# A transformer block on one core: the values group of a step moved behind the last scores, to stand next to the denominators

## The chip, the cores and the metric

The kernel runs on one core of a Trainium2 chip. The metric is the device time of one execution in microseconds. Lower is better. The core's engines each work through their own list of instructions in order and wait for each other by semaphores. PE is TensorE, DVE is VectorE, ACT is ScalarE, POOL is GpSimd, and SP issues the DMAs.

## The reference

The input is x of 4 batches x 2048 tokens x 512 channels. The reference makes a modulation from a small vector, normalizes x, runs causal attention of 16 heads with 32 channels each, and adds the gated result to x:

```python
mod = (_silu(L0_c) @ L0_wmod).reshape(L0_c.shape[0], 6, 1, -1)
sa, ca, ga, sb, cb, gb = (mod[:, 0], mod[:, 1], mod[:, 2], mod[:, 3], mod[:, 4], mod[:, 5])
h = _layernorm(x, axis=-1) * (1 + ca) + sa
# in the attention:
qkv = x @ W_qkv + b_qkv
q = _apply_rope(q, cos, sin); k = _apply_rope(k, cos, sin)
att = jnp.einsum('bhqd,bhkd->bhqk', q, k) / jnp.sqrt(jnp.float32(HS))
att = jnp.where(causal, att, jnp.float32(-1000000000.0))
att = jax.nn.softmax(att, axis=-1)
y = jnp.einsum('bhqk,bhkd->bhqd', att, v)
x = x + ga * (y @ W_proj + b_proj)
```

A second part (layer norm, a routed attention with its own layer norm at the end) follows in the reference. The kernel takes as its inputs only the weights of the first part and the gain and shift of the last layer norm. Each token's row of the output is made from the attention's result by a product with the projection and two normalizations.

## The kernel before

The work of the attention is cut into 16 **stages**: 4 batches x 4 groups of four heads. A stage has two parts.

The **projection part** makes query, key and value of the *next* group: per tile of 128 tokens 12 products on PE (L1060), bias and rotation on DVE and POOL, and a transposition on PE (L1073).

The **step part** is the loop over 40 steps (L1200). A step `s` is a pair `STEPS[s] = (cq, kt)`: 512 query columns (`cq` 0 to 3) against one tile of 128 keys (`kt` from 0 to 4 cq + 3). The last four key tiles of each `cq` are on the diagonal; they are narrower (512, 384, 256, 128 columns) and get a mask product. A step issues on PE:

- four **scores** products, one for each head (L1119), each into one of three banks `ps_scores`. Each waits until ACT has made the exponential (L675) that frees its bank, which is that of three scores before.
- the **values** group of the step before (L1133): four products with 32 output columns each, one per head, into `ps_out`. It waits for all four exponentials of that step.
- the **denominators** of the step before: also groups of four products with 32 columns, into `ps_den`. On the diagonal they read the exponentials (L1156). Off it, POOL adds the exponentials of two steps (`add_pair`, L483) and a **pair-sum** group (L1150) reads the sum, once for two steps. In the last stage there are no pairs, and each step has a group on L1156.
- up to five **maxima** products (`unit_scores`, L1083, with a mask product L1086 on the diagonal): scores of the *next* stage, of which DVE takes the row maxima (L844), so that the exponentials there have their shift. They go through three banks, the `ring`, which also takes the products with the output projection (`proj`, L1105) and the transposed tiles of the next batch (`head_turn`, L1036). A product into the ring waits until DVE has emptied the bank of three uses before.

How many maxima products stand in a step is fixed in advance by `unit_plan`, from a table of loads of PE and DVE. The order within a step is written out by hand in the loop over `place` 0 to 4: scores `place`, then, at certain places, values and denominators, then maxima product `place`. The other engines follow the same loop over steps. ACT makes four exponentials per step, each of which also waits until its `prob` buffer has been used (`prob_used`, three steps deep). ACT also copies finished sums out, and at such times it waits for DVE's reciprocals (L860) and POOL's product (L488). DVE has, between the maxima, the reciprocals, the tiles of the output (`tail_stage`) and the normalizations of the next batch's input (L716, L723, L793). In the last stage nothing comes after, so there are no maxima products, and the output tiles of its own batch are made in it.

`late` is step 1 of a stage that has a next one: there values and denominators come at place 4, after the last tiles' transpositions. Behind a step with `kt` = 0, which opens new sums, values come at place 3. In the other steps they come at place 2.

Of the kernel before, what the change touches and what calls it, by code (L numbers as in the profile page):

```python
# [24 lines left out]
def adaln_block_kernel(nc, x, w_qkv, b_qkv, w_proj, b_proj, ln_g, ln_b, c, w_mod, rope_cos, rope_sin, out):  # L25
# [24 lines left out]
    STEPS = [(cq, kt) for cq in range(NC_) for kt in range(TPC * (cq + 1))]  # L50
# [35 lines left out]
    def tail_at(g, first, last):  # L86
        if first:
            return {}
        if g < 2:
            return {s: g * T0 + k for k, s in enumerate((2, 8, 16, 24, 30))}  # L90
        if g == (2 if last else 3):
            return {s: 2 * T0 + k for k, s in enumerate((2, 8, 14, 20, 26, 30))}
        return {}

    def head_at(g, last):
        return HEAD_AT if g == 2 and not last else {}

    def own_at(g, last):
        return OWN_AT if g == NG - 1 and last else {}
# [19 lines left out]
    def unit_plan(tail, head):  # L119

        fits = lambda r: [min(5, max(0, r * product_load(s, tail, head) - vector_load(s, tail, head))) for s in range(NS)]
        r = 0.0
        while sum(fits(r)) < NS * HG:
            r += 0.01
        plan, k, done = [], 0, 0.0
        for room in fits(r):
            done += room
            upto = min(NS * HG, k + 5, int(done + 0.5))
            plan.append([(i // HG, i % HG) for i in range(k, upto)])
            k = upto  # L130
        assert k == NS * HG
        return plan
# [7 lines left out]
    with ExitStack() as ctx:  # L140
# [125 lines left out]
        def ring_base(b):  # L266

            return NS * HG if isinstance(b, int) and b == 0 else NS * HG + RING * b - NT

        def ring_first(b):  # L270

            return ring_base(b if isinstance(b, int) and b == 0 else 1) % NBK
# [748 lines left out]
        def _(pe):  # L1021
# [10 lines left out]
            def head_turn(b, t, use, n):  # L1032
                pe.wait_ge(head_norm, NT * b + t + 1)
                pe.wait_ge(ring_free, wait_value(use - NBK + 1))
                for k in range(KC):
                    mm = pe.transpose(ring[n % NBK][:, k * P:(k + 1) * P], wk[:, t % 2, k * P:(k + 1) * P], ident[:])  # L1036
                mm.then_inc(ring_full, 1)

            def turn_maxima(G):
                pe.wait_ge(max_split, G + 1)  # L1040
                pe.transpose(ring[0][:, 0:P // 2].bitcast(F16), nm16[:].rearrange("p a n -> p (a n)"),
                             ident16[:]).then_inc(max_turned, 1)

            def qkv(G, g, before, loads):
                pe.wait_ge(wg_ld[g % 2], loads)
                if before is not None:
                    pe.wait_ge(sums_left, NC_ * (before - 1) + NC_)
                for t in range(NT):
                    qkv_tile(G, g, t)
                    if t == 1 and before is not None:  # L1050
                        turn_maxima(before)
                    if t >= 3:
                        turn_tile(G, t - 3)
# [11 lines left out]
            def turn_tile(G, t):  # L1065
                N = NT * G + t
                pe.wait_ge(lo_done, N + 1)
                pe.wait_ge(hi2_done, N + 1)
                pe.wait_ge(tr_evac, wait_value(N - 1))
                for two in range(2):  # L1070
                    for h in range(HG):
                        o = (two * HG + h) * P
                        mm = pe.transpose(ps_tr[t % 2][0:R, o:o + P], qk16[:, t % 3, h, two * R:(two + 1) * R],  # L1073
                                          ident16[:])
                mm.then_inc(qk_tr, 1)
# [34 lines left out]
            def scores(G, par, s, h):  # L1110

                cq, kt = STEPS[s]
                q0 = P * max(kt - TPC * cq, 0)
                w = QC - q0
                diag = kt >= TPC * cq
                k = HG * s + h

                pe.wait_ge(exp_done, wait_value(HG * NS * G + (k - NBK + 1 if k >= NBK else 0)))
                mm = pe.matmul(ps_scores[k % NBK][:, 0:w], qk[0:RM, par, 1, h, kt * P:(kt + 1) * P],  # L1119
                               qk[0:RM, par, 0, h, cq * QC + q0:(cq + 1) * QC], start=True, stop=not diag)  # L1120
                if diag:
                    mm = pe.matmul(ps_scores[k % NBK][:, 0:P], identb[:], mask_kq[:], start=False, stop=True)  # L1122
                mm.then_inc(scores_done, 1)

            def values(G, par, s, paired):

                cq, kt = STEPS[s]
                q0 = P * max(kt - TPC * cq, 0)
                if kt == 0:
                    pe.wait_ge(sums_left, wait_value(NC_ * G + cq))  # L1130
                pe.wait_ge(exp_done, HG * (NS * G + s + 1))
                for h in range(HG):
                    mm = pe.matmul(ps_out[h * HS:(h + 1) * HS, q0:QC], v32[:, par, kt, h * HS:(h + 1) * HS],  # L1133
                                   prob[:, s % 3, h // 2, h % 2, 0:QC - q0], start=kt == 0,
                                   stop=kt == TPC * (cq + 1) - 1)
                if kt < TPC * cq and paired:
                    mm.then_inc(prob_used, 1)
# [39 lines left out]
            def body(b, first, last):  # L1177
                base = ring_base(b)
                n = 0
                bank0 = ring_first(b)  # L1180
                for g in range(NG):
                    G = NG * b + g
                    par = g % 2
                    nxt = not (last and g == NG - 1)
                    if nxt:
                        if g == NG - 1:
                            pe.wait_ge(head_done, NT * (b + 2))

                        qkv(G + 1, (g + 1) % NG, G, 32 * (NG // 2 * b + (g + 1) // 2 + 1))
                        first_evac = NT * (G + 2) - NBK  # L1190
                    else:
                        turn_maxima(G)
                        first_evac = None
                    pe.wait_ge(max_rows, G + 1)
                    pe.wait_ge(max_dma, 32 * (G + 1))
                    if g == 0:
                        pe.wait_ge(scale_rows, 1)
                    tail, head, own = tail_at(g, first, last), head_at(g, last), own_at(g, last)
                    plan = unit_plan(tail, head)
                    for s in range(NS + 1):  # L1200

                        units = plan[s] if s < NS and nxt else []
                        late = s == 1 and nxt
                        for place in range(5):
                            if place < 4 and s < NS:
                                if s == 0 and place < NBK and first_evac is not None:
                                    pe.wait_ge(qkv_evac, first_evac + place + 1)
                                scores(G, par, s, place)
                            if (s, place) in LATE_TURNS and nxt:
                                turn_tile(G + 1, LATE_TURNS[s, place])  # L1210
                            if place == 4 and late:
                                pe.wait_ge(tr_evac, NT * (G + 2))
                            if place == (4 if late else 3 if s > 1 and STEPS[s - 1][1] == 0 else 2) and s > 0:
                                values(G, par, s - 1, nxt)
                            if place == (4 if late else 3) and s > 0:
                                denominators(G, s - 1, nxt)
                            if place < len(units):
                                u, h = units[place]
                                unit_scores(h, u, 1 - par, base + n, bank0 + n)
                                n += 1  # L1220
                        if s in tail or s in own:
                            proj(b if s in own else b - 1, own[s] if s in own else tail[s], base + n, bank0 + n)
                            n += 1
                        if s in head:
                            head_turn(b + 1, head[s], base + n, bank0 + n)
                            n += 1
                return n + bank0
# [43 lines left out]
```

## Time and profile before

| | |
|---|---|
| time, median of 3 runs | 3621.95 us (3618.25 to 3622.92) |
| span of the profiled execution | 3618.4 us (no other time of its own is given) |
| PE busy | 3195.3 us, 88% |
| DVE busy | 2923.3 us, 81% |
| ACT, POOL busy | 1780.1 and 1710.6 us |
| granted TensorE clock, mean | 0.952 |

Busy time is the union of an engine's instructions. A PE product is shown until its results have arrived, so products that follow each other overlap in the rows, and the rate of PE is read from one start to the next. The groups of four products with 32 columns are 8 rows of MATMUL each, since the type is f32, and the timeline merges them to one row with x8. PEld is the load of a product's weights, which stands ahead of it in the queue; it can wait while PE is still busy with earlier products.

### The profile page before, as it was taken

The numbers are of one execution on the slowest core, as the hardware profiler recorded it, in microseconds if no ns is written. First come the engines' busy times: TensorE is split into PE (matmuls) and PEld (weight loads), VectorE is DVE, ScalarE is ACT, GpSimd is POOL, SyncE is SP. The second block draws the span as 40 slices with busy tenths as digits, with TensorE's granted clock in tenths as the row PEclk, the third lists the DMA queues.
The fourth block names the chain that finished last, engine by engine and source line by source line (L and its number), as shares of the span: only waits on it lengthen the run. The fifth ranks groups of instructions, "written<-read, shape, count | busy, mean of one in ns | idle before, by whom it ended". The sixth has DMA issues, their size and how long they took to land.

```text
span 3618.4 us, 69458 instructions
## 1 busy us (share of the span) xinstructions
PE 3195.3 (88%) x22176; PEld 1266.8 (35%) x22176; DVE 2923.3 (81%) x5670; ACT 1780.1 (49%) x3667; POOL 1710.6 (47%) x1385
## 2 busy tenths in 40 slices
PE   3699999999989989888988989989888999999895
PEld 1324343424343332434334243333424334243221
DVE  4797777897778888898878878888888888888676
ACT  3306565555645454564535545465444545544451
POOL 2403435373526455373653626455363554626454
PEclk8759999999999999999999999999999999999897
DMA  6000000110011000110111001010011010001022
GB/s 213 12 12 4 18 8 7 35 36 15 10 41 40 24 25 27 30 42 21 40 33 41 31 18 42 27 31 25 27 42 47 30 36 21 27 19 36 19 91 73
DMA packets 112229, 124.62 MB, mean 34 GB/s; under 512 B 18276, under 2 KB 85092, under 8 KB 110708
## 3 DMA queue, kind: packets, MB, share of 16 engines
q1 hardware_dynamic: 111864, 120.07, 10.5%
q8 instruction: 190, 3.11, 0.4%
q14 instruction: 175, 1.43, 0.1%
HBM read 83.02 MB, written 36.50 MB: 33 GB/s over the span
## 4 chain that ended last, share of the span: by engine, by line
PE 40%; DVE 31%; issue 13%; DVEq 6%; ACT 2%; POOLq 2%; POOL 2%; DMA 0%; ACTq 0%; SPq 0%
PE ring L1083 10%; DVE mpart L844 9%; PE ps_out L1133 9%; PE ps_scores L1119 7%; PE ps_den L1150 4%; DVE qk L821 4%; PE ps_den L1156 3%; PE ring L1105 3%; DVE wk L888 3%; DVE qk L807 2%; DVE ropeB L829 2%; DVE qk L816 2%; PE ps_scores L1060 2%; DVE dsum L860 2%; DVEq L838 1%
## 5 line engine op out<-in xcount | busy, mean ns | idle before, releaser
L675 ACT ACTIVATE prob<-ps_scores 128x512 f32<-128x512 f32 (+3 forms) x2560 | 1265.7, 537 | 1105.7 <-PE ps_scores L1122 535.0
L844 DVE TENSOR_REDUCE mpart<-ring 128x1 f32<-128x512 f32 (+3 forms) x2560 | 1403.0, 599 | 335.0 <-PE ring L1086 181.7
L483 POOL TENSOR_TENSOR psum<-prob 128x1024 f32<-128x1024 f32 x360 | 866.8, 2429 | 325.5 <-ACT prob L675 163.0
L1083 PE MATMUL ring<-qk 96*128 96x512 f16 (+3 forms) x2560 | 892.3, 368 | 118.1 <-DVE mpart L844 106.3
L1119 PE MATMUL ps_scores<-qk 98*128 98x512 f16 (+3 forms) x2560 | 879.2, 357 | 57.5 <-ACT prob L675 53.6
L1133 PE MATMUL ps_out<-prob,v 128*32 128x512 f32 (+3 forms) x5120 | 609.4, 548 | 6.6 <-ACT qk L635 6.6
L1083 PEld LDWEIGHTS ring<-qk 96*128 96x128 f16 x2560 | 239.7, 99 | 943.8 <-DVE mpart L844 704.4
L1060 PE MATMUL ps_scores<-wg,hT 128*128 128x384 f16 x3072 | 538.3, 328 | 22.9 <-ACT osum L702 9.9
L465 POOL TENSOR_TENSOR ropeA<-qk,cos_sb 128x256 f32<-128x256 f32 x256 | 200.5, 783 | 750.1 <-DVE v L810 745.2
L1119 PEld LDWEIGHTS ps_scores<-qk 98*128 98x128 f16 x2560 | 248.4, 99 | 364.0 <-ACT prob L675 232.9
L1060 PEld LDWEIGHTS ps_scores<-wg,hT 128*128 128x128 f16 x3072 | 292.2, 98 | 200.7 <-issue 18.9
L630 ACT CAST qk<-qk 128x128 f16<-128x128 f32 x256 | 76.2, 298 | 378.1 <-DVE qk L816 378.1
L860 DVE RECIPROCAL dsum<-dsum 128x128 f32<-128x128 f32 x252 | 234.7, 937 | 18.9 <-ACT osum L702 17.6
L1086 PE MATMUL ring<-mask_qk,identb 128*128 128x128 bf16 x1024 | 233.2, 230 | 0.0
L1122 PE MATMUL ps_scores<-mask_kq,identb 128*128 128x128 bf16 x1024 | 229.6, 226 | 0.0
L1105 PE MATMUL ring<-wp,otin 128*128 128x512 f16 x756 | 187.7, 399 | 41.6 <-DVE mpart L844 28.0
L1156 PE MATMUL ps_den<-prob,ones 128*32 128x512 f32 (+3 forms) x2240 | 216.8, 459 | 0.0
L1150 PE MATMUL ps_den<-psum,ones 128*32 128x512 f32 x1440 | 208.5, 620 | 2.2 <-POOL psum L483 2.2
L513 POOL TENSOR_TENSOR x<-wk,xs 128x512 f32<-128x512 f32 x48 | 61.3, 1277 | 309.1 <-DVE wk L873 309.1
L807 DVE SCALAR_TENSOR_TENSOR qk<-ps_scores,bg 128x256 f32<-128x256 f32 x256 | 108.8, 425 | 98.5 <-PE ps_scores L1060 57.9
L821 DVE TENSOR_TENSOR qk<-qk 128x128 f16<-128x128 f32 x256 | 179.4, 701 | 1.2
L453 POOL TENSOR_TENSOR vare<-mv,eps_t 128x1 f32<-128x1 f32 x192 | 54.5, 284 | 245.3 <-DVE mv L718 89.8
(127 smaller groups left out, 3134.9 us busy)
## 6 DMA issues: line engine op xcount, KB each, us to landing
xs<-in_L_attn_x_dram SPq DMA_DIRECT2D x124, 256.0 KB, 2.8
attn_out_T<-ot SPq DMA_DIRECT2D x63, 256.0 KB, 2.2
otin<-attn_out_T SPq DMA_DIRECT2D x30, 512.0 KB, 4.6
out_dram<-x SPq DMA_DIRECT2D x60, 256.0 KB, 2.1
wg<-w_qkv_halves SPq DMA_DIRECT2D x16, 768.0 KB, 5.2
qk<-in_L_wmod_dram SPq DMA_DIRECT2D x1, 6144.0 KB, 27.1
bc<-modulation SPq DMA_DIRECT2D x4, 1536.0 KB, 9.1
hT<-in_L_attn_W_qkv_dram SPq DMA_DIRECT2D x1, 3072.0 KB, 10.4
```

Source lines behind the costliest of these rows:

```text
L483: pool.tensor_tensor(psum2[:, p], prob[:, s % 3, p], prob[:, (s + 1) % 3, p], ALU.add).then_inc(pair_sum, 1)
L675: act.activation(prob[:, s % 3, p, h % 2, 0:w], ps_scores[(HG * s + h) % NBK][:, 0:w], ACT.Exp, scale=SCALE).then_inc(exp_done, 1)
L821: dve.tensor_tensor(qk16[:, u, :, 2 * HS:3 * HS], ropeR[:, u, :, 0, :], qk16[:, u, :, 0:HS], ALU.subtract)
L844: dve.tensor_reduce(mpart[:, h, qt, kc:kc + 1], ring[n % NBK][:, 0:w], AX.X, ALU.max).then_inc(ring_free, 1)
L860: dve.reciprocal(dsum[:, cols], dsum[:, cols]).then_inc(recip_done, 1)
L1060: mm = pe.matmul(ps_scores[(t + SHIFT) % NBK][:, 0:GW], hT[:, a, k, t * P:(t + 1) * P], wg[:, g % 2, w, k, :], start=(i == 0), stop=(i == ...
L1083: mm = pe.matmul(ring[n % NBK][:, 0:w], qk[0:R, par, 0, h, qt * P:(qt + 1) * P], qk[0:R, par, 1, h, kc * QC:kc * QC + w], start=True, stop ...
L1105: mm = pe.matmul(ring[n % NBK][:, :], att, wp16[:, w, k, :], start=(i == 0), stop=(i == 3 * NG - 1))
L1119: mm = pe.matmul(ps_scores[k % NBK][:, 0:w], qk[0:RM, par, 1, h, kt * P:(kt + 1) * P], qk[0:RM, par, 0, h, cq * QC + q0:(cq + 1) * QC], st ...
L1133: mm = pe.matmul(ps_out[h * HS:(h + 1) * HS, q0:QC], v32[:, par, kt, h * HS:(h + 1) * HS], prob[:, s % 3, h // 2, h % 2, 0:QC - q0], start ...
L1150: mm = pe.matmul(ps_den[h * HS:(h + 1) * HS, :], ones[:], psum2[:, h // 2, h % 2, :], start=kt == 2, stop=False)
L1156: mm = pe.matmul(ps_den[h * HS:(h + 1) * HS, q0:QC], ones[:], prob[:, s % 3, h // 2, h % 2, 0:QC - q0], start=kt == 0, stop=kt == TPC * (c ...
```

## The change

The values group is called at the place of the denominators, directly ahead of them, in all steps: place 3, or place 4 in the late step.

```diff
@@ -1210,9 +1210,8 @@
                                 turn_tile(G + 1, LATE_TURNS[s, place])
                             if place == 4 and late:
                                 pe.wait_ge(tr_evac, NT * (G + 2))
-                            if place == (4 if late else 3 if s > 1 and STEPS[s - 1][1] == 0 else 2) and s > 0:
+                            if place == (4 if late else 3) and s > 0:
                                 values(G, par, s - 1, nxt)
-                            if place == (4 if late else 3) and s > 0:
                                 denominators(G, s - 1, nxt)
                             if place < len(units):
                                 u, h = units[place]
```

PE's list in step 27 of a stage with maxima products (third group of a batch in the loop over batches), before. L1119 is scores, L1083 a maxima product, L1133 values, L1150 pair sums; `psum2` holds the sums of pairs:

```order
L1083 MATMUL ring0<-qk 128x512 [waits ring_free]
L1118 REGISTER_ALU
L1119 MATMUL ps_scores2<-qk 128x512 [waits exp_done]
L1131 ISA
L1133 MATMUL ps_out<-prob,v32 32x512 [waits exp_done]
L1133 MATMUL ps_out<-prob,v32 32x512 x3
L1082 REGISTER_ALU
L1083 MATMUL ring1<-qk 128x512 [waits ring_free]
L1118 REGISTER_ALU
L1119 MATMUL ps_scores0<-qk 128x512 [waits exp_done]
L1149 ISA
L1150 MATMUL ps_den<-psum2,ones 32x512 [waits pair_sum]
```

The same place on PE with the change:

```order
L1083 MATMUL ring0<-qk 128x512 [waits ring_free]
L1118 REGISTER_ALU
L1119 MATMUL ps_scores2<-qk 128x512 [waits exp_done]
L1082 REGISTER_ALU
L1083 MATMUL ring1<-qk 128x512 [waits ring_free]
L1118 REGISTER_ALU
L1119 MATMUL ps_scores0<-qk 128x512 [waits exp_done]
L1131 ISA
L1133 MATMUL ps_out<-prob,v32 32x512 [waits exp_done]
L1133 MATMUL ps_out<-prob,v32 32x512 x3
L1149 ISA
L1150 MATMUL ps_den<-psum2,ones 32x512 [waits pair_sum]
```

The third maxima product and the fourth scores product now stand ahead of the values group, which stands directly ahead of the pair sums.

PE's list in steps 28 and 29 of the last stage, which has no maxima products, before:

```order
L1119 MATMUL ps_scores1<-qk 128x512 [waits exp_done]
L1119 MATMUL ps_scores2<-qk 128x512 [waits exp_done]
L1119 MATMUL ps_scores0<-qk 128x512 [waits exp_done]
L1133 MATMUL ps_out<-prob,v32 32x512 [waits exp_done]
L1133 MATMUL ps_out<-prob,v32 32x512 x3
L1119 MATMUL ps_scores1<-qk 128x512 [waits exp_done]
L1156 MATMUL ps_den<-prob,ones 32x512 x4
```

The same with the change:

```order
L1119 MATMUL ps_scores1<-qk 128x512 [waits exp_done]
L1119 MATMUL ps_scores2<-qk 128x512 [waits exp_done]
L1119 MATMUL ps_scores0<-qk 128x512 [waits exp_done]
L1119 MATMUL ps_scores1<-qk 128x512 [waits exp_done]
L1133 MATMUL ps_out<-prob,v32 32x512 [waits exp_done]
L1133 MATMUL ps_out<-prob,v32 32x512 x3
L1156 MATMUL ps_den<-prob,ones 32x512 x4
```

Here the four scores products follow each other without anything between them. DVE, ACT, POOL and SP have the same lists as before.

## Rows read from the trace of the kernel before

**Rows 1.** The page: busy shares of the engines, and the chain that ended last.
```profile
PE 3195.3 (88%) x22176; PEld 1266.8 (35%) x22176; DVE 2923.3 (81%) x5670; ACT 1780.1 (49%) x3667; POOL 1710.6 (47%) x1385
...
PE 40%; DVE 31%; issue 13%; DVEq 6%; ACT 2%; POOLq 2%; POOL 2%; DMA 0%; ACTq 0%; SPq 0%
```

**Rows 2.** Windows (PE, PEld, DVE, ACT, POOL busy): plain, product, head step part; last stage.
```profile
483.00:627.00 144.00, 137.31 (x1025) 46.52 (x1026) 106.52 (x193) 89.24 (x181) 66.34 (x33) 0.99 0.03 9
1275.00:1448.00 173.00, 154.98 (x1084) 54.57 (x1084) 143.92 (x238) 89.38 (x182) 97.04 (x68) 0.98 0.08 27
1490.00:1656.00 166.00, 147.37 (x1090) 55.38 (x1088) 150.44 (x306) 99.64 (x198) 97.46 (x81) 0.99 0.10 30
3415.00:3618.00 203.00, 162.38 (x1052) 48.89 (x1050) 129.56 (x188) 80.98 (x171) 89.55 (x103) 0.88 0.24 75
```

**Rows 3.** Waits (total, times, longest) in the product and the head step part.
```profile
PEld ring L1083 <- DVE mpart L844: 43.9, 58, 3.1
PE ring L1083 <- DVE mpart L844: 8.5, 11, 2.2
...
PEld ring L1083 <- DVE mpart L844: 43.8, 60, 2.2
PE ring L1083 <- DVE mpart L844: 10.9, 14, 1.7
```

**Rows 4.** Timeline of PE (start, duration): plain stage, steps 27, 28; a values-denominators join.
```profile
578.44 1.06 PE L1133 MATMUL ps_out<-prob,v 128*32 128x512 f32 x8
579.44 0.39 PE L1083 MATMUL ring<-qk 96*128 96x512 f16 x1
...
580.98 0.60 PE L1083 MATMUL ring<-qk 96*128 96x512 f16 x2
...
582.15 0.39 PE L1083 MATMUL ring<-qk 96*128 96x512 f16 x1
582.38 0.38 PE L1119 MATMUL ps_scores<-qk 98*128 98x512 f16 x1
582.69 1.06 PE L1133 MATMUL ps_out<-prob,v 128*32 128x512 f32 x8
583.69 0.39 PE L1083 MATMUL ring<-qk 96*128 96x512 f16 x1
583.92 0.60 PE L1119 MATMUL ps_scores<-qk 98*128 98x512 f16 x2
...
1500.91 1.06 PE L1133 MATMUL ps_out<-prob,v 128*32 128x512 f32 x8 [0.47 <-ACT qk L635]
1501.79 1.05 PE L1156 MATMUL ps_den<-prob,ones 128*32 128x512 f32 x8
```

**Rows 5.** Timeline of PE, last stage: step 13 (kt before is 0), step 14.
```profile
3453.02 0.81 PE L1119 MATMUL ps_scores<-qk 98*128 98x512 f16 x3
3454.09 0.39 PE L1119 MATMUL ps_scores<-qk 98*128 98x512 f16 x1 [0.26 <-ACT prob L675]
...
3456.27 0.82 PE L1119 MATMUL ps_scores<-qk 98*128 98x512 f16 x3
...
3459.34 0.39 PE L1105 MATMUL ring<-wp,otin 128*128 128x512 f16 x1
```

**Rows 6.** Timeline of DVE in the plain stage beside rows 4.
```profile
577.25 0.69 DVE L844 TENSOR_REDUCE mpart<-ring 128x1 f32<-128x512 f32 x1 [0.69 <-PE ring L1083]
...
580.71 3.18 DVE L844 TENSOR_REDUCE mpart<-ring 128x1 f32<-128x512 f32 x5
```

**Rows 7.** Timelines of PE and DVE in a head stage, steps 27 and 28.
```profile
1603.14 0.39 PE L1083 MATMUL ring<-qk 96*128 96x512 f16 x1 [0.21 <-DVE x L793]
...
1604.68 0.60 PE L1083 MATMUL ring<-qk 96*128 96x512 f16 x2
...
1606.49 0.39 PE L1083 MATMUL ring<-qk 96*128 96x512 f16 x1 [0.99 <-DVE mpart L844]
...
1604.95 0.94 DVE L860 RECIPROCAL dsum<-dsum 128x128 f32<-128x128 f32 x1
```

## The prediction

> **What bounds the kernel now.** I read the page's shares first [rows 1]: PE is busy 88% of 3618.4 us and DVE 81%, ACT, POOL and DMA far less, and the chain that ended last is 40% PE, 31% DVE and 13% "issue", so two engines share the bound and the question is which has it where. The windows by stage [rows 2] answer that. A stage is one group of four heads; it has a projection part, which the change leaves alone, and a step part, which it touches. I name the step parts by what DVE has beside its row maxima:
> - plain (3 of the 16): 144 us, PE 137.3 busy, DVE 106.5: PE alone sets the pace;
> - product (9): 173 us and more, PE 155.0, DVE 143.9: now one, now the other;
> - head (3): 166 us, PE 147.4, DVE 150.4: mostly DVE;
> - the last one: 203 us with the end of the kernel, no maxima.
>
> The waits [rows 3] say the same. The weight load of a maxima product stands still for DVE 43.9 us in a product and 43.8 us in a head stage, but PE itself was idle for it only 8.5 and 10.9 us. The difference is what other PE work, the values group among it, covers. That cover is what the change moves.
>
> **What the change removes: switches of PE.** Values, pair sums and denominators are groups of four products with 32 output columns; all else on PE here has 128. The start-to-start times in [rows 4] give the price of going from one to the other. Maxima to scores, both with 128 output columns, is 0.23 us (582.15 to 582.38). Scores to a values group is 0.31 (582.38 to 582.69). A values group to a product with 128 output columns is 1.00 (582.69 to 583.69). A values group to a denominators group right behind it is 0.88 (1500.91 to 1501.79). So going in costs about 0.31 - 0.22 = 0.09 us (two scores in a row are 0.22 apart: the row at 583.92 holds two, 0.60 us together and 0.38 each) and coming out 1.00 - 0.88 = 0.12, and a join of two groups saves one of each: 0.21 us.
>
> The Trainium skill has two rules on it that do not agree. "TensorEngine Tiling (Array Packing)", section Key Properties, says that a change of tiling mode drains the engine; "TensorE: Matmul & The Clock Gate", section Step-by-step, says that the next matmul's fill overlaps the drain of the one before, so that a stream costs its columns alone. By the second there is nothing to save in a switch and the sum below has only its losses. The rows speak for the first, with 0.09 and 0.12 us.
>
> **How many joins.** Of the 40 steps of a stage, the first keeps its place, and so do the three behind a step with kt = 0, and the closing call has nothing between its two groups. That leaves 35 moved values groups. In 15 stages denominators of key tiles off the diagonal are made from pair sums, once in two steps, so only 23 of the 35 have a group to join (14 on the diagonal, 9 with a pair alone). The other 12 only move past one scores and one maxima product. In the last stage there are no pairs, the step after the first moves too, and all 36 join. 15 x 23 + 36 = 381 joins, 381 x 0.21 = 80 us, 2.2% of the span, if nothing stood against it. No wait is added; the semaphores are those of before. But PE goes through its list in order, so a maxima or scores product that has to wait now holds up values and denominators, which used to run in that time.
>
> **The cover that goes, last stage.** Between scores 2 and scores 3 there is nothing left there, and scores 3 needs the bank that exponential 0 of its own step frees. The trace has this order already, in the steps behind kt = 0 [rows 5]: scores 0 to 2 at 3453.02, scores 3 only at 3454.09, idle for ACT, then values and denominators joined, next step at 3456.27: 3.25 us. The next step, in the old order, goes from 3456.27 to 3459.34: 3.07 us. So a wide step loses 0.40 us of cover for a join of 0.21, and is 0.18 us longer. With some 24 wide steps, and nothing for the narrow ones (a shorter exponential, a shorter cover), this is +4.5 us; I take +5. Ends: 0, if the product tiles between the steps keep setting the time, and +10, if the joins give nothing there (24 x 0.40).
>
> **Plain stages.** [Rows 4] begin in a step with a pair group, the next has none, and [rows 6] are DVE beside them. The third maxima product comes at 579.44, 1.00 us behind values at 578.44. In the new order it stands where values stood, at 578.35 since it needs no switch; its bank was freed by the maximum that ended at 577.94. Scores 3 follow at 578.57, values at 578.88, pair sums at 579.76 and the fourth maxima product at 580.76, where it was 580.98. The join pays in full. In the following step the second maxima product (582.15) waited for DVE already and stays where it is. The third could go at 582.60 and needs the bank of the one issued behind 580.98; its maximum is the third in DVE's unbroken row of five of 0.64 us each, so the bank is free at about 582.7. Values go near 583.2, where they were at 582.69, but the third maxima and scores 3 are then behind PE, and the next step, which began at 584.14 with the second product of the row at 583.92, begins at about 584.2. The gain of 0.22 is gone. Not every step is that full. So of 23 x 0.21 = 4.8 us I keep half: -2.4 per stage, -7 for three. Ends -4.8 and +1 each.
>
> **Head stages.** In [rows 7] PE has the third maxima product at 1603.14, idle 0.21 us for DVE although the values group went right before it. In the new order it still waits for 1603.14 and nothing hides that: PE stands for some 1.3 us. Scores 3 follow at 1603.37, values at 1603.68, pair sums at 1604.56, and the fourth maxima product comes at 1605.56 where it was 1604.68, 0.88 us late. But DVE reaches that one only after its reciprocal (1604.95 + 0.94) and the third maximum, and at 1606.49 PE was idle 0.99 us for DVE anyway. The lateness ends there. With one of 16 tiles in every second step I take this for 20 of 23 joins: nothing lost, nothing won, 0 per stage. Ends: -4.8, and +10 if the 0.73 us of a mean wait (43.8 / 60) less the 0.21 is lost in each of the 20.
>
> **Product stages.** Five or six tiles, with two to three steps of heavy DVE work each, so about 11 of the 23 joins stand as in the head stages (0) and 12 as in the plain ones (0.10 each): -1.2, for nine -11. Ends -4.8, and +6 if the 0.76 us of a mean wait (43.9 / 58) less 0.21 is lost in each of 11.
>
> **Sum.** -7 + 0 - 11 + 5 = -13 us. This is against the profiled execution, whose span of 3618.4 us is the only time of its own that is given, within the 3618.25 to 3622.92 of the timed runs. So it is within their scatter, what lies around the span adds nothing that can be told, and I take the difference from the median: 3622 - 13 = 3609 us. By the rule that a drain costs nothing only the +5 of the lost cover would be left, 3627; with the 0.31 and the 1.00 against 0.88 in the rows I give that no chance of its own.
>
> **Rivals.**
> - DVE takes it all. For it: DVE is 81% busy over the whole and 91% in the head stages, and the number of maxima per step is fixed by a plan that the change does not touch. Against it: 74% in a plain stage (106.5 of 144). The joins give nothing but in a few narrow steps, and 3620 us comes out, no change.
> - The cover is worth more than the switch. A maxima or scores product that waits now keeps values and denominators standing in its queue, and the time is not given back by a later wait that shrinks. The place is the third maxima product of steps in product and head stages. The upper ends above make 9 x 6 + 3 x 10 = 84 us of lateness. It decides the sign once a quarter of that survives to the next values group (13 + 7 us against 84); with a third of it, 28 us, +5 in the last stage and nothing won elsewhere it is 3655 us. For it: the gain lost again in [rows 4, 6]; a longer block of 2.2 us without a maxima product, against three banks of 0.69 us each. Against it: the wait at 1606.49.
> - The joins are paid nearly in full, -50 us, 3572 us, if DVE, which gets its third tile a microsecond earlier, frees banks earlier too. Against it: its order of work is fixed and it is already behind where it is waited for.
> - TensorE's clock: the windows of [rows 2] have a granted clock of 0.98 to 0.99 and the last stage 0.88, a mean over the upper level of 2.4 GHz and the lower of 1.2. PE now stands still for longer at a time in some steps, and each 10 us that it works at the lower level instead of the upper cost 5. I give it no case of its own; it is one reason for a wide range.
>
> **How the numbers follow.** This kernel's measurement can tell about 0.2%, 7 us, from no change. Forecast (the joins pay in part, 3609) 0.40; DVE takes it 0.22; cover lost 0.32; nearly full gain 0.06. The forecast's own range is 3590 to 3618, and about a tenth of its chance is too small to tell. With the full gain, faster is 0.42; same 0.26; slower 0.32. The range takes in most of the lost cover and half of the full gain: 3572 to 3655.
>
> **What would show it.** Right: pair-sum and denominators groups start 0.88 us behind values groups; a plain step part is 2 to 3 us shorter than 144, a head part the same within 2 us, wide steps of the last stage 3.25 us. Wrong: PE's own idle time for DVE at the maxima line doubles in product and head stages and their step parts grow (cover lost); a join that costs 1.00 us as before (no saving); plain parts unchanged with DVE waits on PE in them grown.

## The result

The changed kernel takes 3627.5 us (median of 20 runs, 3620.2 to 3634.9) against 3622.6 us before (20 runs, 3617.5 to 3626.7). The ratio is 1.0017, with a 95% interval of 1.001 to 1.0023: slower by 0.17%, some 5 us. The forecast was 3609 us.

The page of the changed kernel, busy shares and the chain that ended last, to lay beside [rows 1]:

```profile
PE 3149.2 (87%) x22176; PEld 1315.1 (36%) x22176; DVE 2912.4 (80%) x5670; ACT 1754.9 (48%) x3667; POOL 1708.2 (47%) x1385
...
PE 38%; DVE 32%; issue 13%; DVEq 6%; ACT 3%; POOLq 2%; POOL 2%; DMA 0%; ACTq 0%; SPq 0%
```

PE is busy 46 us less in a span that is 5 us longer. So the joins did save time on PE, and more than that went into waits. The mean granted clock is 0.952 in both, which hides that it went down in some stages and up in others. The windows say where. Those of the changed kernel run from the end of one projection part to the start of the next (plain, product, head), under them the same windows of the kernel before (columns as in [rows 2]):

```profile
478.40:617.20 138.80, 133.11 (x1027) 50.54 (x1026) 105.22 (x194) 87.92 (x182) 66.31 (x33) 0.99 0.03 9
1262.70:1439.30 176.60, 155.41 (x1087) 57.99 (x1084) 144.04 (x239) 88.55 (x182) 96.89 (x68) 0.96 0.08 27
1481.20:1648.60 167.40, 144.43 (x1091) 58.51 (x1088) 148.10 (x306) 98.49 (x198) 97.52 (x81) 0.99 0.09 30
```
```profile
482.60:626.90 144.30, 137.52 (x1027) 46.45 (x1026) 106.92 (x194) 89.54 (x182) 66.34 (x33) 0.99 0.03 9
1274.70:1448.10 173.40, 155.28 (x1087) 54.59 (x1086) 144.32 (x239) 89.72 (x182) 97.04 (x68) 0.98 0.08 27
1490.00:1656.50 166.50, 147.37 (x1090) 55.38 (x1088) 150.58 (x306) 100.13 (x198) 97.46 (x81) 0.99 0.10 30
```

The plain stage is 5.5 us shorter, the product stage 3.2 longer, with a granted clock of 0.96 for 0.98, and the head stage 0.9 longer. Summed over all 16, from the first scores product of a stage to that of the next: plain -15.1, head +2.6, product +19.2, last stage with the end of the kernel -2.7 us, and +1.4 ahead of the first. The -2.7 is mostly not the change's: the last stage is 1.7 to 3.1 us shorter also in the traces of experiments 1 and 3 that leave it as it was.

**The join.** In a plain stage of the changed kernel (PE, start and duration) values come at 570.43, pair sums 0.88 us later, the next maxima 0.98 after that:

```profile
569.90 0.38 PE L1083 MATMUL ring<-qk 96*128 96x512 f16 x1
570.12 0.38 PE L1119 MATMUL ps_scores<-qk 98*128 98x512 f16 x1
570.43 1.07 PE L1133 MATMUL ps_out<-prob,v 128*32 128x512 f32 x8
571.31 1.04 PE L1150 MATMUL ps_den<-psum,ones 128*32 128x512 f32 x8
572.29 0.61 PE L1083 MATMUL ring<-qk 96*128 96x512 f16 x2
...
573.69 0.38 PE L1119 MATMUL ps_scores<-qk 98*128 98x512 f16 x1
574.06 0.39 PE L1083 MATMUL ring<-qk 96*128 96x512 f16 x1
574.29 0.38 PE L1119 MATMUL ps_scores<-qk 98*128 98x512 f16 x1
```

**The step that lost.** Step 21 of a product stage, PE, of the changed kernel. Its first scores product (scores 0) stands at 1350.06:

```profile
1351.13 0.22 PE L1122 MATMUL ps_scores<-mask_kq,identb 128*128 128x128 bf16 x1
1354.28 0.45 PE L1083 MATMUL ring<-qk 96*128 96x512 f16 x1 [2.93 <-DVE mpart L844]
1354.52 0.53 PE L1119 MATMUL ps_scores<-qk 98*128 98x384 f16 x1
1354.84 0.31 PE L1122 MATMUL ps_scores<-mask_kq,identb 128*128 128x128 bf16 x1
1355.09 1.93 PE L1133 MATMUL ps_out<-prob,v 128*32 128x512 f32 x8
1356.80 1.58 PE L1150 MATMUL ps_den<-psum,ones 128*32 128x512 f32 x8
1358.20 1.03 PE L1156 MATMUL ps_den<-prob,ones 128*32 128x512 f32 x8
1359.16 0.39 PE L1083 MATMUL ring<-qk 96*128 96x512 f16 x1
```

and DVE there:

```profile
1350.83 2.68 DVE L888 SCALAR_TENSOR_TENSOR wk<-wk,rstd,bc 128x512 f32<-128x512 f32 x1
1353.66 2.08 DVE L844 TENSOR_REDUCE mpart<-ring 128x1 f32<-128x384 f32 x4 [0.15 <-issue]
1359.59 0.69 DVE L844 TENSOR_REDUCE mpart<-ring 128x1 f32<-128x512 f32 x1 [3.85 <-PE ring L1083]
```

The same step before, PE (scores 0 at 1363.17):

```profile
1367.32 0.39 PE L1083 MATMUL ring<-qk 96*128 96x512 f16 x1 [1.87 <-DVE mpart L844]
...
1367.86 1.06 PE L1150 MATMUL ps_den<-psum,ones 128*32 128x512 f32 x8
1368.74 1.04 PE L1156 MATMUL ps_den<-prob,ones 128*32 128x512 f32 x8
1369.72 0.60 PE L1083 MATMUL ring<-qk 96*128 96x512 f16 x2
```

The third maxima product goes 4.2 us into the step in both kernels, since DVE is held by L888 of an output tile. Before, values lay within that wait. Now they lie behind it, in front of pair sums *and* denominators, since the key tile of step 20 is the first on the diagonal. Two things follow. DVE has taken all that was there and stands 3.85 us for the next maxima product, so nothing gives the lateness back. And the groups take 1.71 and 1.40 us where a join takes 0.88: behind the unbroken wait PE works at the lower clock. The windows of step 21 in the six product stages with five tiles, of the changed kernel, tell the two apart (columns as above; the clock is third from the right):

```profile
1133.13:1141.12 7.99, 4.99 (x44) 1.90 (x41) 5.55 (x7) 1.85 (x4) 2.97 (x2) 1.00 0.09 31
1350.06:1359.61 9.55, 6.62 (x44) 2.18 (x41) 5.48 (x7) 1.85 (x4) 2.90 (x2) 0.82 0.27 82
2013.11:2024.03 10.92, 7.92 (x43) 2.27 (x40) 5.53 (x7) 1.85 (x4) 2.96 (x2) 0.69 0.06 21
2232.16:2240.09 7.93, 4.99 (x44) 1.91 (x41) 5.49 (x7) 1.85 (x4) 2.91 (x2) 1.00 0.32 101
2887.20:2897.88 10.68, 7.90 (x44) 2.22 (x40) 5.40 (x7) 1.92 (x4) 2.83 (x2) 0.68 0.05 19
3105.56:3114.45 8.89, 6.39 (x44) 2.07 (x41) 5.13 (x7) 1.92 (x4) 2.55 (x1) 0.81 0.26 79
```

Before, all six have a clock of 1.00 and 6.86 to 7.07 us, 41.8 in all, as these two do:

```profile
1363.17:1370.16 6.99, 5.12 (x41) 1.77 (x40) 5.41 (x7) 2.35 (x5) 2.83 (x2) 1.00 0.37 112
2017.94:2025.01 7.07, 5.12 (x42) 1.78 (x40) 5.49 (x7) 2.35 (x5) 2.91 (x2) 1.00 0.08 30
```

Now they are 56.0. Where the clock stays up, the step costs 0.9 us more. Where part of it is at 1.2 GHz, 2.0 to 3.9. The wait of PE ahead of the third maxima product is 2.50 to 3.00 us in the six, and 3.00 and 2.94 us in the two that keep the clock, so its length alone does not tell which step loses it.

### The profile page after: what moved, and what is told of

It is laid out like the page before. It is cut to its first block, busy times and chain, and to the rows that moved or that the text cites. A ratio compares the mean times of both kernels' runs of the same rounds, so it can differ in the third digit from the quotient of the medians.

```text
span 3623.7 us, 69458 instructions
## 1 busy us (share of the span) xinstructions
PE 3149.2 (87%) x22176; PEld 1315.1 (36%) x22176; DVE 2912.4 (80%) x5670; ACT 1754.9 (48%) x3667; POOL 1708.2 (47%) x1385
## 4 chain that ended last, share of the span: by engine, by line
PE 38%; DVE 32%; issue 13%; DVEq 6%; ACT 3%; POOLq 2%; POOL 2%; DMA 0%; ACTq 0%; SPq 0%
DVE mpart L844 10%; PE ring L1083 9%; PE ps_out L1133 9%; PE ps_scores L1119 6%; DVE qk L821 4%; PE ps_den L1150 3%; PE ring L1105 3%; PE ps_den L1156 3%; DVE wk L888 3%; DVE qk L807 2%; DVE ropeB L829 2%; DVE qk L816 2%; PE ps_scores L1060 2%; DVE dsum L860 2%; DVE wk L886 2%
## 5 line engine op out<-in xcount | busy, mean ns | idle before, releaser
L675 ACT ACTIVATE prob<-ps_scores 128x512 f32<-128x512 f32 (+3 forms) x2560 | 1239.0, 539 | 1098.1 <-PE ps_scores L1122 531.2
L844 DVE TENSOR_REDUCE mpart<-ring 128x1 f32<-128x512 f32 (+3 forms) x2560 | 1391.3, 598 | 355.1 <-PE ring L1086 184.4
L1083 PE MATMUL ring<-qk 96*128 96x512 f16 (+3 forms) x2560 | 890.6, 368 | 159.2 <-DVE mpart L844 115.2
L1119 PE MATMUL ps_scores<-qk 98*128 98x512 f16 (+3 forms) x2560 | 880.4, 356 | 77.3 <-ACT prob L675 71.1
L1133 PE MATMUL ps_out<-prob,v 128*32 128x512 f32 (+3 forms) x5120 | 613.8, 552 | 5.8 <-ACT qk L635 5.8
L1083 PEld LDWEIGHTS ring<-qk 96*128 96x128 f16 x2560 | 236.5, 99 | 810.5 <-DVE mpart L844 556.8
L1119 PEld LDWEIGHTS ps_scores<-qk 98*128 98x128 f16 x2560 | 251.5, 99 | 384.8 <-ACT prob L675 225.8
L1150 PE MATMUL ps_den<-psum,ones 128*32 128x512 f32 x1440 | 208.2, 619 | 0.0
```

The lines of the kernel that those rows point to most:

```text
L675: act.activation(prob[:, s % 3, p, h % 2, 0:w], ps_scores[(HG * s + h) % NBK][:, 0:w], ACT.Exp, scale=SCALE).then_inc(exp_done, 1)
L844: dve.tensor_reduce(mpart[:, h, qt, kc:kc + 1], ring[n % NBK][:, 0:w], AX.X, ALU.max).then_inc(ring_free, 1)
L1083: mm = pe.matmul(ring[n % NBK][:, 0:w], qk[0:R, par, 0, h, qt * P:(qt + 1) * P], qk[0:R, par, 1, h, kc * QC:kc * QC + w], start=True, stop ...
L1150: mm = pe.matmul(ps_den[h * HS:(h + 1) * HS, :], ones[:], psum2[:, h // 2, h % 2, :], start=kt == 2, stop=False)
```

## Experiments

All are measured beside the kernel before, on the same chip. Ratios are to before, with their 95% intervals.

**1. The change in one kind of stage alone.** One condition differs; that of the plain stages:

```diff
-if place == (4 if late else 3 if s > 1 and STEPS[s - 1][1] == 0 else 2) and s > 0:
+if place == (4 if late else 3 if (nxt and not tail and not head) or (s > 1 and STEPS[s - 1][1] == 0) else 2) and s > 0:
     values(G, par, s - 1, nxt)
```

Plain stages:

> The change in the three plain stages alone. The per-step comparison of the two traces has 5.0 us less in each of them (step part and the boundary behind it), so 3622 - 15 = 3607 us, if stages add up. Rival: what the plain stages gain is given back at the boundary or in the stages behind them, 3618 us or more.

Measured: 3610.3 us, ratio 0.9965 (0.9953 to 0.9977), so -12 us.

Product stages (`3 if tail or ...`):

> The change in the product stages alone (those with output tiles of the batch before). If the loss sits there: slower by 15 to 22 us, 3637 to 3644 us, more than the whole change. Rival (loss spread over all stages, or in the head and the last stage): within 5 us of before.

Measured: 3636.6 us, 1.0035 (1.0021 to 1.0048), +14 us.

Last stage (`3 if not nxt or ...`):

> The change in the last stage alone: 0.19 us more in each wide step and 0.07 in each narrow one, 3.7 us: 3626 us. The traces of before and of the change differ there by -1.6 us, since three stretches at the lower clock are missing in the change; if that comes from the order of the last stage and not by chance, it is 3621 us.

Measured: 3625.0 us, 1.0004 (0.9995 to 1.0013): +2 us, which is not told from none. Its wide steps have the pattern and the 3.26 us that was read off [rows 5]; here step 14 of the changed kernel, with its product tile from 3466.80:

```profile
3463.54 0.82 PE L1119 MATMUL ps_scores<-qk 98*128 98x512 f16 x3
3464.62 0.39 PE L1119 MATMUL ps_scores<-qk 98*128 98x512 f16 x1 [0.26 <-ACT prob L675]
3464.94 1.07 PE L1133 MATMUL ps_out<-prob,v 128*32 128x512 f32 x8
3465.82 1.04 PE L1156 MATMUL ps_den<-prob,ones 128*32 128x512 f32 x8
3466.80 2.76 PE L1105 MATMUL ring<-wp,otin 128*128 128x512 f16 x12
```

The parts add up to +7 us (-12 + 14 + 2, and the head stages' 2.6), and the whole is +5, so they add up within what such sums can tell. The loss is in the product stages.

**2. The lossy steps alone put back.** The change, with values at place 2 in two steps of each product stage (the edit is shown against the kernel before):

```diff
+if place == (4 if late else 2 if tail and s in ((21, 35) if g < 2 else (19, 35)) else 3) and s > 0:
     values(G, par, s - 1, nxt)
```

> The whole change, but in two steps of each product stage (21 and 35, or 19 and 35 in those with six tiles) values stay at place 2. Theory 1 (in these steps the third maxima product waits 2 to 3 us for DVE, values used to fill that wait, and PE's clock falls in the unbroken wait): 18 of some 700 calls moved back give 20 to 28 us: 3600 to 3607 us. Rival (waits of DVE's long operations would move to the next step): 3620 us or more.

Measured: 3604.8 us, 0.9949 (0.9935 to 0.9962). Eighteen calls out of the 561 that the change moves turn +5 us into -18. In its trace fifteen of them do it; in step 35 of the three stages with six tiles nothing comes back (+4.5 us against before, +4.1 in the change), and 6 says why.

**3. The clock apart from the cover.** The change, with eight products more in the same steps, ahead of the third maxima product. Their results are overwritten by scores 3.

```diff
+if place == 2 and tail and nxt and s in ((21, 35) if g < 2 else (19, 35)):
+    k3 = HG * s + 3
+    pe.wait_ge(exp_done, wait_value(HG * NS * G + k3 - NBK + 1))
+    for _ in range(8):
+        pe.matmul(ps_scores[k3 % NBK][:, :], qk[0:RM, par, 1, 3, 0:P],
+                  qk[0:RM, par, 0, 3, 0:QC], start=True, stop=True)
 if place < len(units):
```

> The whole change, with eight extra scores products in steps 19, 21 and 35 of the product stages, into the bank that scores 3 overwrites, right behind scores 2. They fill 1.7 of the 3.0 to 3.4 us in which PE waits there, add nothing to the result, and keep PE at work. If a good part of the change's loss in these steps is PE's clock at its lower level behind the wait (0.93 us lost in step 21 where the clock stays up, 2.0 to 3.9 us where it falls): 3610 to 3617 us, and step 21 longer than before by 0.9 us in all six stages. If it is the lost cover alone: 3627 us or more.

Measured: 3596.0 us, 0.9926 (0.9912 to 0.9939). Work that nobody needs makes the changed kernel 31 us faster, more than either expectation. Step 21 of the same stage, PE (L1221 are the extra products):

```profile
1348.83 1.89 PE L1221 MATMUL ps_scores<-qk 98*128 98x512 f16 x8
1351.97 0.39 PE L1083 MATMUL ring<-qk 96*128 96x512 f16 x1 [1.24 <-DVE mpart L844]
...
1352.51 1.06 PE L1133 MATMUL ps_out<-prob,v 128*32 128x512 f32 x8
1353.39 1.04 PE L1150 MATMUL ps_den<-psum,ones 128*32 128x512 f32 x8
1354.25 1.04 PE L1156 MATMUL ps_den<-prob,ones 128*32 128x512 f32 x8
```

The maxima product still goes 4.3 us into the step; the groups are back at 0.88 and 0.86. All six windows of step 21 have a clock of 1.00 and 7.6 to 8.0 us, 47.1 in all, and the two in which the change had kept its clock without them took 7.99 and 7.93, so the extra products do nothing there but hold the clock. So of the 14.1 us that the change lost in step 21, 5.2 are the cover (47.1 - 41.8, 0.9 a step) and 8.9 the clock. Step 19 gives back 5.8 us and step 35 of the stages with five tiles 10.7, with the clock at 1.00 there too. Not all of the 31 us is the clock, however: 5.7 come from step 35 of the stages with six tiles, where the clock was up already. That is a second thing, under 6.

The same products in the order of before, behind values and ahead of the third maxima product:

> The order of before with the same eight extra products in steps 19, 21 and 35 of the product stages, behind the values group and ahead of the third maxima product, where PE waits 2 us more. The clock is at its lower level in step 35 of five of the nine product stages of before; if the extra products keep it up there: 5 x 1.5 = 8 us less, 3614 us, and the change with them (3596) is 18 us ahead of it: that is what joining is worth with the clock alike. If the extra products helped the change in another way than by the clock (pair sums of POOL pushed past DVE's long operations), it is 3605 us or less.

Measured: 3603.1 us, 0.995 (0.9936 to 0.9964). The expectation had given 3605 us or less to another way than the clock. The trace does not show that way: DVE's long operations are as before (L888 takes 2.69 us and L934 0.75 on median in both). It shows the clock, at more places than I had counted. Steps 35 and 36 together of one product stage, before and with the extra products:

```profile
1423.44:1434.73 11.29, 9.11 (x51) 2.75 (x50) 9.17 (x13) 4.60 (x9) 6.88 (x4) 0.85 0.00 1
```
```profile
1421.32:1431.04 9.72, 9.37 (x59) 3.23 (x58) 9.05 (x13) 4.60 (x9) 6.55 (x4) 1.00 0.01 2
```

In all nine product stages it is so: a clock of 0.85 to 0.87 and 105.6 us before, 1.00 and 91.6 us now. The product stages as a whole get 12 us shorter, and 5 more go in other stages, where nothing was altered. With the extra products in both, the change is ahead by about 7 us, not by the 18 that I expected. This pair ran on two chips and its intervals just touch.

**4. Which cover is it?** Three orders of the same pieces, each shown by its main lines. `usual` is true in the late step, in step 1 of the last stage and behind a step with `kt` = 0, which keep their order. Joined between the third maxima product and scores 3 (scores 3 keeps its cover, the maxima product does not):

```diff
     unit_scores(h, u, 1 - par, base + n, bank0 + n); n += 1    # place 2
+if place == 2 and not usual:
+    values(G, par, s - 1, nxt)
+    denominators(G, s - 1, nxt)
```

> Joined groups between the third maxima product and scores 3: only scores 3 keeps its cover. Theory 1: the losses of 1 to 3.9 us at steps 19, 21 and 35 of product stages stay, the last stage gains 36 x 0.21 = 7 us instead of losing 5; about 3615 to 3622 us. Theory 2: as fast as with both covers, 3580 to 3590 us.

Measured: 3654.2 us, 1.0097 (1.0082 to 1.0111). Joined behind scores 3, the third maxima product behind the groups:

```diff
+for k in ([place] if usual else {2: [], 3: [2, 3]}.get(place, [place])):   # after values and denominators
```

> Joined groups behind scores 3 and ahead of the third maxima product: only the maxima product keeps its cover. Theory 1: the losses at steps 19, 21 and 35 of the product stages are gone, but two maxima products now follow each other behind the block; 3595 to 3605 us, wide steps of the last stage 3.25 us as in the change. Theory 2: as slow as the change, 3622 to 3630 us.

Measured: 3630.6 us, 1.0027 (1.0017 to 1.0037). Values alone moved behind the third maxima product, nothing joined:

> Only the values group moves, behind the third maxima product and ahead of scores 3, denominators stay behind scores 3: no join, the maxima product's cover gone, that of scores 3 kept. Theory 1: slower than the change by what the joins gave, 15 to 30 us: 3640 to 3655 us, plain stages no shorter than before. Theory 2: as fast as before, 3622 us. Theory 3: same as the change but for the last stage, about 3620 us.

Measured: 3687.3 us, 1.0185 (1.0172 to 1.0198).

In the product stages, against before and counted as above, the sums with joined groups are: +19 us with neither covered (the change), +26 with scores 3 covered (e2), -18 with the maxima product covered (e3), -33 with both (5 below). Uncovered and unjoined it is +44 (e4). So it is the maxima product's cover, worth 37 us in the change's order, while covering scores 3 alone wins nothing. All three totals missed what was expected all the same. In e3 the head stages got 25 us longer. e2 is 27 us behind the change and e4 60, and both have less of the clock (granted mean 0.943 and 0.946 for 0.952): over the span that is up to 34 and 25 us, by an estimate from these means. What is left of e4's 60 us, 35 or more, is 0.09 us or more for each of 381 joins, so it does not show that a join is worth more than 0.21. Why these orders have more stretches at the lower clock was not tried.

**5. Both groups at place 2.** The join and both covers:

```diff
-if place == (4 if late else 3) and s > 0:
+if place == (4 if late else 3 if s > 1 and STEPS[s - 1][1] == 0 else 2) and s > 0:
     denominators(G, s - 1, nxt)
```

> Values and denominators joined, but at place 2, ahead of the third maxima product and scores 3, so that the join is kept and both covers too. Theory 1 (the change lost its gain because the third maxima product waits for DVE with values, pair sums and denominators queued behind it): clearly faster than before, 381 joins x 0.21 us = 80 us at most, about 40 us after what DVE takes back: 3582 us, and no step of a product stage longer by over 0.6 us. Theory 2 (the loss is scores 3 waiting for ACT): the same here, faster by 25 to 50 us. Theory 3 (a join saves less than 0.21 us in this place): 3615 us or more. If the pair sums are not ready yet at place 2, waits of the pair-sum group for POOL appear, and the gain is halved.

Measured: 3622.0 us, 1.0002 (0.999 to 1.0014), single runs from 3605 to 3635. The expectation failed as a total. Product stages get 33 us shorter, head stages 39 longer. To see if it is the order in the head stage itself:

> Both groups at place 2 in the three head stages alone. The trace with both at place 2 everywhere has 12 to 15 us more in each head stage: 3661 us if that is the order in the head stage itself, DVE's normalization (L723) longer on mean than 0.87 us, since it runs beside POOL's pair sums. If it came from the stages ahead: 3622 us.

Measured: 3655.4 us, 1.0092 (1.0076 to 1.0107). It is. From scores 0 of step 0 to scores 0 of step 39 the third head stage of this kernel takes 174.9 us for 161.6, with a clock of 0.95 for 0.99, and its normalizations on DVE are longer; the window, then the row of L723 there, which had 903 ns on mean before:

```profile
2377.98:2552.93 174.95, 145.42 (x1038) 57.30 (x1037) 152.59 (x296) 96.03 (x191) 98.25 (x81) 0.95 0.10 28
...
L723 DVE TENSOR_SCALAR wk<-xs,mv,rstd 128x512 f32<-128x512 f32 x16 | 20.3, 1269 | 0.3 <-POOL rstd L455 0.2
```

That is 5.8 us of DVE's time and some stretches at the lower clock. Which of the two starts the other wasn't tried.

**6. Each stage in the order that suits it.** Plain stages as in the change, product stages with both groups at place 2, head and last stage as before:

```diff
+if place == (4 if late else 3 if (nxt and not tail and not head) or (s > 1 and STEPS[s - 1][1] == 0) else 2) and s > 0:
     values(G, par, s - 1, nxt)
+if place == (4 if late else 2 if tail and nxt and s > 1 and STEPS[s - 1][1] != 0 else 3) and s > 0:
     denominators(G, s - 1, nxt)
```

> Each kind of stage with the order that was best for it: plain as in the change, product with both groups joined at place 2, head and last stage as before. If the parts add up: -15 (plain), -33 (product), 0 (head, last): 3574 us. Rival: stages are coupled through the clock and POOL, and half is lost: 3598 us.

Measured: 3568.7 us, 0.985 (0.9835 to 0.9865): 54 us faster than before and the best version of all.

A side effect of the order shows in step 35 of product stages with six tiles. It is 1.3 to 1.4 us longer in the change at the full clock, and there PE has no wait for DVE ahead of the third maxima product. DVE of the changed kernel, then POOL:

```profile
1854.18 0.75 DVE L932 SCALAR_TENSOR_TENSOR wk<-wk,mv,bc 128x512 f32<-128x512 f32 x1
1855.00 2.67 DVE L934 SCALAR_TENSOR_TENSOR x<-wk,rstd,xs 128x512 f32<-128x512 f32 x1
...
1854.68 5.19 POOL L483 TENSOR_TENSOR psum<-prob 128x1024 f32<-128x1024 f32 x2 [1.20 <-PE ps_den L1150]
```

and the same with the extra products:

```profile
1847.93 0.75 DVE L934 SCALAR_TENSOR_TENSOR x<-wk,rstd,xs 128x512 f32<-128x512 f32 x1
...
1848.64 2.34 POOL L483 TENSOR_TENSOR psum<-prob 128x1024 f32<-128x1024 f32 x1 [2.23 <-PE ps_den L1150]
```

Before, it was the other of the two that was long:

```profile
1860.02 2.61 DVE L932 SCALAR_TENSOR_TENSOR wk<-wk,mv,bc 128x512 f32<-128x512 f32 x1
1862.71 0.75 DVE L934 SCALAR_TENSOR_TENSOR x<-wk,rstd,xs 128x512 f32<-128x512 f32 x1
```

The same DVE operation takes 0.75 us, or 2.67 when POOL's addition has started before it. The Trainium skill, "SBUF — State Buffer", section Who interferes with whom, has it that a VectorE instruction with two SBUF inputs contends with a GpSimd instruction that reads SBUF, and that the order of issue decides who blocks. The rows agree. Scores 3, 1.4 us earlier in the change, bring POOL's additions earlier, and they then meet L934, and L886 of the step before (2.56 us for 0.74), in place of L932. Of L886, L888, L932 and L934 three are slowed where it was two.

## Why the prediction was wrong

- **A join saves 0.21 us: right.** In the join above pair sums stand 0.88 us behind values, where values ahead of a product with 128 output columns take 1.00 [rows 4]. And from step 2 on each of the three plain stages is 4.1 to 4.3 us shorter for its 23 joins, 0.18 each. By the second of the two rules that the prediction took from the Trainium skill ("TensorE: Matmul & The Clock Gate", section Step-by-step: fill and drain overlap) there would have been nothing. That the sum by this rule was 3627, and 3627 was measured, is chance: the joins did pay, and the product stages lost it elsewhere.
- **Plain stages -7 us, upper end of the gain -4.8 each: too cautious.** -15.1 by the traces, -12 measured alone. I had worked out one pair of steps in which the gain is taken back, and halved the whole by it. In the changed kernel the next step does wait a little in such a place (from 573.69 to 574.06 it is 0.37 us, for 0.23 in the pair behind it), but the joins pay 0.18 of the 0.21 us on the mean. The rest of the 15.1 is 1.3 to 1.4 us each in steps 0 and 1 of two stages, which hold a stretch at the lower clock at another place than before; the third has nothing there. So 12.4 us are the joins.
- **Head stages 0: right** within 1 us each (+0.9). The third maxima product goes uncovered and a later wait takes it up. The sign that was named for lost cover, PE's idle time for DVE at the maxima line doubled, did not show in the product stages either (8.5 us in the window before, 10.3 in the change): it is a sum, and the loss sits in few steps.
- **Last stage +5: the mechanism right to 0.01 us, the sum not told from 0.** 0.19 us more in a moved wide step and 0.07 in a narrow one, wherever the clock is alike in both traces; the granted clock of that stage moves by more than that (0.88 and 0.90).
- **Product stages -11: this is the step that failed.** It came out at +19 us. The prediction treated the waits there as in the head stages ("nothing lost") and the rest as half plain. The rest is right: all steps but 18 did get 12 us shorter in sum, for 11 forecast. Those 18, step 21 of the six stages with five tiles, step 19 of the three with six and step 35 of all nine, sum to +31.5 us (14.1, 6.2 and 11.2), 4.1 of it from step 35 of the stages with six tiles, where DVE's operations meet POOL's. What I had not asked is what stands *behind* a wait and what DVE has left to do in it. In the head step of [rows 7] DVE had a reciprocal and a maximum to go; in step 21 it had nothing, stood 3.85 us, and PE was the late one.
- **The clock "no case of its own": wrong.** It was named, and put at some width of the range. It is 8.9 of the 14.1 us of step 21, and with the extra products the change is at 3596 us. The trace of before had the sign of it: waits of 1.7 to 2.4 us ahead of the third maxima product in 14 of these 18 executions, with values issued ahead of them, and in steps 35 and 36 a stretch at the lower clock in all nine product stages. Taking values out made the waits 2.5 to 3.0.
- **The rival of the lost cover had the right side and place** (third maxima product), for product stages, not for head stages. It gave 3655, and 3627 was measured, since the plain stages paid more than it allowed and the lateness of most steps did not survive. What it did not have is the clock.

That 5 us come out is a balance of -15 and +19, and not the absence of an effect.

## What to carry to other kernels

Before moving work out of a wait on an engine that goes in order, look at each long wait on its own: what fills it, what stands behind it, and whether the engine that is waited for has other work in that time. A sum of average waits over a stage hides the two steps that decide. On TensorE a wait that is filled can be worth more than the work in it, since the clock behind it is at stake (8.9 us against 5.2 in step 21 here); and where stages differ in what bounds them, try one order per kind of stage.

## What the runs showed of the hardware

- Eight needless products of 0.22 us each, in a wait of 2.5 to 3.0 us, kept the granted clock at 1.00 in six of six places where it had been 0.68 to 0.82 in four, and the kernel got 31 us faster, some 25 of it in steps where the clock came back. In the order of before they took steps 35 and 36 from 0.85 to 0.87 to 1.00 in nine of nine stages, 105.6 to 91.6 us.
- One DVE operation with 512 columns (L934) takes 0.75 us, or 2.67 us when it starts while POOL adds 1024 columns. DVE's maxima (L844), which read PSUM, do not change: none of the 2560 takes over 0.70 us.
- Values, pair sums and denominators, each of four products with 32 columns, stand 0.86 to 0.88 us apart at the full clock, and 0.96 to 1.00 us ahead of a product with 128 output columns; at the lower clock 1.71 us apart.
